# Decoder kernel of four layers: steps 20 to 37 of the closing chain one to four slots closer, last mixture opened at slot 90 instead of 94

## The reference, cut to what matters

```python
x = x + L2_xattn(layernorm(x), ctx, ctx)      # 16 heads, softmax, one output weight
x = x + L2_ffn(layernorm(x))                  # gated; fp4 quantised input, hidden and weights
x = x + L3_attn(layernorm(x))                 # linear: x @ q.T @ (x.T @ x)
x = x + L3_xattn(layernorm(x), ctx, ctx, ...) # no softmax, so keys x values is one 128x128; inner layernorm
x = x + L3_ffn(layernorm(x))                  # mixture: 8 experts 128 -> 512 -> 128, top 2 of 8, gelu
```

## Time and profile before

| what | us |
|---|---|
| median of three runs | 1243.61 (1237.75 to 1248.25) |
| the profiled execution | 1246.88 |
| its span in the trace | 1245.6 |
| outside the span | 1.3 |
| PE busy | 1028.6 (83%) |
| DVE busy | 800.2 (64%) |
| ACT busy | 612.5 (49%) |
| POOL busy | 252.0 (20%) |

### The profile page before, as it was taken

The page is one execution under the profiler, slowest core; times in us unless marked ns, Lnnn a source line. Parts: engine busy times, 40 slices in busy tenths (PEclk is TensorE's granted clock), DMA queues, the critical chain, the costliest instruction groups (busy, mean ns, idle before and its releaser), DMA issues.

```text
span 1245.6 us, 19903 instructions
## 1 busy us (share of the span) xinstructions
PE 1028.6 (83%) x7630; PEld 550.0 (44%) x7649; DVE 800.2 (64%) x2016; ACT 612.5 (49%) x1018; POOL 252.0 (20%) x309
## 2 busy tenths in 40 slices
PE   5777779999899974778867889999658868779999
PEld 4233313333667652345532333566412333437767
DVE  7786867751324467877777882677688887665412
ACT  2456436566433527678763777323115546433342
POOL 2833210000000225477551000001222001000000
PEclk9778869999999996566776997999858989879999
DMA  8323040000000210068013201700101200100000
GB/s 302 94 72 85 27 179 2 2 2 2 1 1 1 77 54 7 1 186 156 17 45 125 116 2 19 125 1 1 52 26 33 97 1 2 34 1 1 1 9 9
DMA packets 34785, 61.23 MB, mean 49 GB/s; under 512 B 4771, under 2 KB 25076, under 8 KB 33092
## 3 DMA queue, kind: packets, MB, share of 16 engines
q1 hardware_dynamic: 33828, 58.64, 16.7%
q10 hardware_dynamic: 864, 1.33, 0.3%
HBM read 42.91 MB, written 16.65 MB: 48 GB/s over the span
## 4 chain that ended last, share of the span: by engine, by line
PE 59%; DVE 27%; ACT 5%; issue 4%; POOL 3%; DMA 2%; SPq 1%; DVEq 0%; POOLq 0%; ACTq 0%
PE ps_s L879 10%; PE ps_e L869 9%; PE ps_v L672 6%; DVE mx L1864 6%; PE ps_e L608 5%; PE ps_s L629 3%; PE ps_e L606 3%; DVE ps_s L1860 2%; PE ps_e L973 2%; PE ps_s L960 2%; ACT work L1396 2%; DVE mx L1854 2%; DVE stats L1802 1%; DVE xn L1820 1%; PE ps_v L1144 1%
## 5 line engine op out<-in xcount | busy, mean ns | idle before, releaser
L1396 ACT ACTIVATE work<-ps_e 128x512 f32<-128x512 f32 x448 | 250.7, 598 | 148.1 <-PE ps_e L608 142.8
L2622 POOL TENSOR_TENSOR rstd<-rstd,halves 128x2 f32<-128x2 f32 x52 | 36.6, 704 | 699.0 <-DVE rstd L1807 698.8
L1864 DVE TENSOR_REDUCE mx<-ps_s 128x2 f32<-128x1024 f32 x128 | 154.1, 1222 | 27.8 <-PE ps_s L629 26.3
L629 PE MATMUL ps_s<-ctx_stack,q_stack 49*128 49x512 bf16 (+1 forms) x384 | 128.5, 453 | 47.1 <-DVE mx L1864 34.8
L608 PE MATMUL ps_e<-q_stack,ctx_stack 52*128 52x256 bf16 (+1 forms) x768 | 149.7, 297 | 16.8 <-issue 6.3
L1498 ACT ACTIVATE work<-ps_s,keep 128x512 f32<-128x512 f32 x136 | 93.1, 687 | 140.4 <-PE ps_s L879 137.5
L672 PE MATMUL ps_v<-work,vaug 128*32 128x256 f32 x1536 | 132.0, 420 | 4.8 <-ACT work L1384 4.8
L869 PEld LDWEIGHTS ps_e<-ffn_w,work 128*128 128x128 f32 x960 | 117.9, 196 | 21.0 <-issue 19.9
L879 PE MATMUL ps_s<-xnT,ffn_w 128*128 128x512 f32 x240 | 119.4, 623 | 3.6 <-ACT work L1498 3.6
L869 PE MATMUL ps_e<-ffn_w,work 128*128 128x128 f32 x960 | 119.7, 280 | 0.8 <-DVE x L2054 0.8
L2064 DVE SCALAR_TENSOR_TENSOR x<-ps_e,gates,x 128x128 f32<-128x128 f32 x128 | 38.9, 346 | 121.7 <-PE ps_e L869 118.7
(11 more groups left out here) (380 smaller groups left out, 1815.7 us busy)
## 6 DMA issues: line engine op xcount, KB each, us to landing
q_stack<-q_scr SPq DMA_DIRECT2D x32, 192.0 KB
ffn_w<-in_L0f_w SPq DMA_DIRECT2D x1, 4608.0 KB, 14.7
ffn_w<-in_L1f_w SPq DMA_DIRECT2D x1, 3456.0 KB, 13.1
q_scr<-parts SPq DMA_DIRECT2D x16, 192.0 KB, 2.1
c_scr<-ffn_w SPq DMA_DIRECT2D x12, 256.0 KB, 7.7
kx_scr<-ffn_w SPq DMA_DIRECT2D x12, 256.0 KB, 4.2
ctx_stack<-kx_scr SPq DMA_DIRECT2D x2, 1536.0 KB
ctx_stack<-c_scr SPq DMA_DIRECT2D x2, 1536.0 KB
```

Of the source, the lines that this page charges most:

```text
L629: return pe.matmul(ps_s[i][:, parity, :], q_stack[p0:p0 + n_rows, b, pair, part * P:(part + 1) * P], ctx_stack[p0:p0 + n_rows, pair, b * S ...
L1396: act.activation(pt[:, parity, :, :].rearrange("p k q -> p (k q)"), bank[f"e{parity}"], ACT.Exp).then_inc(exped, 1)
L1864: m = dve.tensor_reduce(mx[:, b, :, pair, part], ps_s[i][:], AX, ALU.max, negate=True)
```

## The change

A table STEP_AT gives each step its distance to the close slot. Steps up to 18 keep theirs; 20 to 37 come one to four slots sooner, 22 in the slot of 21. `chain_steps` goes by the table, and so do all counts. TAIL0 goes from 94 to 90, and every piece of the mixture comes four slots sooner. Since the cross attention still has steps in slots 90 to 92 (the close of batch 3), `l3_tail` now calls `cross_slot` too, behind the slot's pieces and ahead of its chain, with s1 alone.

```diff
+STEP_AT = {4: 4, 5: 5, 7: 7, 8: 8, 9: 9, 10: 10, 11: 11, 12: 12, 15: 15, 16: 16, 17: 17, 18: 18, 20: 19, 21: 20,
+           22: 20, 24: 21, 25: 22, 27: 23, 28: 24, 29: 25, 30: 26, 31: 27, 32: 28, 33: 29, 34: 30, 35: 31, 36: 32, 37: 33}
 CHAIN = [("L2f", 3), ("L3a", 17), ("L3x", 24), ("L3x-inner", 33), ("L3f", 34)]
-tail = sorted((close_slot(X2, b) + at, b, st) for st, at in CHAIN for b in range(B))
-tail = [(st, b) for _, b, st in tail]
+
+def chain_slot(b, at):
+    return close_slot(X2, b) + STEP_AT.get(at, at)
+
+tail = sorted((chain_slot(b, at), st != "L2f", b, at, st) for st, at in CHAIN for b in range(B))
+tail = [(st, b) for _, _, b, _, st in tail]
...
-LAST = {A0: 54, X0: 96, X1: 96, X2: 93, "chain": 125}
+LAST = {A0: 54, X0: 96, X1: 96, X2: 93, "chain": 121}
...
-TAIL0 = 94
+TAIL0 = 90
...
-PIECES_BEFORE = {95: 2, 96: 1, 97: 1, 98: 1, 99: 2, 101: 1, 102: 1, 103: 1, 104: 1, 105: 1, 106: 1, 107: 1, 108: 1, 109: 1,
...
+PIECES_BEFORE = {91: 2, 92: 1, 93: 1, 94: 1, 95: 2, 97: 1, 98: 1, 99: 1, 100: 1, 101: 1, 102: 1, 103: 1, 104: 1, 105: 1,
...
     def chain_steps(slot):
         for b in range(B):
-            yield b, slot - close_slot(X2, b)
+            for at in STEP_AT:
+                if chain_slot(b, at) == slot:
+                    yield b, at
...
                 n += PIECES_BEFORE.get(t, 0)
+                if t < LAST[X2]:
+                    cross_slot(X2, t, kp("L2x_T"), None, window_tile)
                 chain(t)
```

More of the change, by code:

```diff
@@ L140 @@
 TURNS = [("L2f", 7), ("L3a", 20), ("L3x", 27), ("L3f", 36)]
-turned_tail = sorted((close_slot(X2, b) + at, b, st) for st, at in TURNS for b in range(B))
-TURN_AT = order_of(front + [(st, b) for _, b, st in turned_tail])
+turned_tail = sorted((chain_slot(b, at), b, at, st) for st, at in TURNS for b in range(B))
+TURN_AT = order_of(front + [(st, b) for _, b, _, st in turned_tail])
 BEFORE = {"L2f": "L2x", "L3a": "L2f", "L3x": "L3a", "L3f": "L3x"}
@@ L150 @@
 CHAIN_PS = [17, 20, 22, 24, 33]
-PS_AT = order_of([(at, b) for _, b, at in sorted((close_slot(X2, b) + at, b, at) for at in CHAIN_PS for b in range(B))])
-LAST = {A0: 54, X0: 96, X1: 96, X2: 93, "chain": 125}
+PS_AT = order_of([(at, b) for _, b, at in sorted((chain_slot(b, at), b, at) for at in CHAIN_PS for b in range(B))])
+LAST = {A0: 54, X0: 96, X1: 96, X2: 93, "chain": 121}
 CFILL = {X0: 32, X1: 128, X2: 192}
@@ L231 @@
 ROUTE1 = len(PIECES) - 2
-PIECES_BEFORE = {95: 2, 96: 1, 97: 1, 98: 1, 99: 2, 101: 1, 102: 1, 103: 1, 104: 1, 105: 1, 106: 1, 107: 1, 108: 1, 109: 1,
-                 110: 1, 111: 1, 113: 1, 114: 2, 116: 1, 117: 1, 118: 1, 120: 1, 122: 2, 123: 2, 124: 1}
+PIECES_BEFORE = {91: 2, 92: 1, 93: 1, 94: 1, 95: 2, 97: 1, 98: 1, 99: 1, 100: 1, 101: 1, 102: 1, 103: 1, 104: 1, 105: 1,
+                 106: 1, 107: 1, 109: 1, 110: 2, 112: 1, 113: 1, 114: 1, 116: 1, 118: 2, 119: 2, 120: 1}
 L3F_OWN = 6
@@ L1538, in l3_tail @@
                 chain(t, False)
+                if t < LAST[X2]:
+                    cross_slot(X2, t, None)
                 chain(t, True)
@@ L2118, in l3_tail @@
                 n += PIECES_BEFORE.get(t, 0)
+                if t < LAST[X2]:
+                    cross_slot(X2, t, "L2f", window_tile)
                 chain(t)
```

## The result

The changed kernel takes 1253.32 us (median of 15 runs, 1249.97 to 1259.84), the kernel before beside it 1243.61 (15 runs, 1236.35 to 1254.59). The ratio is 1.0084, interval 1.0065 to 1.0104: slower by about 9.7 us. The forecast was 1242.9 with a range up to 1251, so both the value and the range were wrong, on the slow side. The profiled execution has a span of 1253.0 us, and PE's clock was granted at 0.864 on average.

A forecast was written before the change was run, and what follows sets the result against it. PE was taken as the bound from 1122.77 us on, with idle time and low clock to win between 1045 and 1123. Terms 0 + 1.0 - 3.2 + 1.5 = -0.7 us gave 1242.9 against the median 1243.61; range 1234 to 1251.

The forecast's parts named there:

- Slots 59 to 68: Batch 0 moved, DVE paced by the maxima, up to F': value 0, a wait of 0.8 us gone or come.
- F' to F: From batch 1's fp4 end (F') to batch 2's (F), slots 68 to 84: +1.0 us, from waits at steps 36 and 27.
- the 0.81 of the root is covered: Part of F' to F: with step 28 leaving DVE's fp4 block (0.60), it gives back 1.4 us.
- F to the first downs: From batch 2's fp4 end until twelve ups, gates and bias are done: F + 38.75 instead of F + 41.97, so -3.2 us.
- That clock held for 11.35 us of work; I take the same here: Step in F to the first downs: 11.35 us of work at the low clock, as before, 5.65 in full-speed units.
- From there to the end: Behind the first downs: waits of 2.3 us in slot 104 and 0.5 in slot 108, old waits gone; net +1.5 us.
- A third gap, and slower: Rival at L554 behind step 35 of batch 2, slot 104: clock falls there too, +7.4 us, 1251.0; chance 0.17.
- The clock stays up: Rival in slot 88: the wait is too short to drop the clock, -7.9 us, 1235.7; chance 0.17.
- The slots count: Rival in the tail: batch 3's chain, not PE's work, sets it; four slots fewer give -10.7 us, 1232.9; chance 0.06.
- signs of a wrong forecast: Clock under 1.00 behind the first downs, first up later than F + 15, or period between fp4 ends under 35 us.
- signs of being right: Step 36 waits 4 to 5 us in slots 72 and 88, DVE's holes gone, first up near F + 12, bias about 3.

The follow-up runs named there:

- Filled: Changed kernel with idle matmuls only ahead of the turns of step 27 (2 for batch 0, 4 for batch 1): 1247.14 us, ratio 1.0033.
- At one clock: Changed kernel with five waits filled by 29 idle matmuls (1240.99 us) beside the kernel before with its waits over 1 us behind slot 70 filled (1238.25 us).
- the filled kernel: Changed kernel, same order, with 29 idle matmuls in five waits (step 36 of batches 0, 1, 2; step 27 of batch 1; bias): 1240.99 us, ratio 0.9983.
- the experiment on before: Kernel before with idle matmuls at two waits only, 5 and 11 at the turns of step 36 of batches 0 and 1: 1243.89 us, ratio 1.0009.
- three other runs: Changed kernel with steps 27 to 37 one slot later (1240.22 us), with only step 27 filled (1247.14 us), with only step 36 filled (1247.71 us).

## Why the prediction was wrong, point by point

- *What bounds the kernel.* Right in the place: the difference arose almost wholly where PE has slack and a clock below 1.00. Its clock was named there, but I had read it from long stretches and so missed two of its four falls. The mechanism, waits that move and a clock that falls at them, was the right one; their sizes and number were not.
- *Slots 59 to 68: value 0, bounds ±0.8.* The stretch up to F' grew by 2.0 us. What failed is "PE wants the normalised tile of step 25 one slot after DVE makes it instead of two", priced as a wait of at most 0.8 with nothing for the clock. It came as 1.00 + 0.47, inside a fall that had begun at the maxima and that lasted 10.3 us instead of 3.6. Filled, the stretch is +0.2 (46.31 against 46.13).
- *F' to F: +1.0, bounds -1.4 and +3.4.* This is the term that failed most: +6.45. At one clock the order costs +2.8, inside the bounds, so taking the middle was 1.8 too low. Two of its parts were wrong. Step 36's wait was forecast at 4.1 and was 2.68, near the old 2.49: the turn came 6.70 us behind F', as counted (6.55), but PE was occupied for 4.0 us of it and not 2.5, as the sum had left out its wait of 1.02 for ACT's lift. And "the 0.81 of the root is covered", a gain, came as two more uncovered roots, 1.6 us of DVE's waits. Step 27's wait, up to 1.8, was 2.07. The other 3.6 us are the clock, which I had priced at nothing: the second wait of the period, in slot 79, lets it fall once more.
- *F to the first downs: -3.2, bounds -8.9 and +1.5.* It came as -0.5. The first up was forecast near F + 12 and stands at F + 11.74, the bias wait was forecast at 3.2 and is 3.41. The step "That clock held for 11.35 us of work; I take the same here" failed in form: the first fall held for 7.5 us of work, and a second one, behind the bias wait (1114.4 to 1121.2), for 6.2 more. In its sum it was nearly right: the clock's price was put at 5.65 us, and filling the waits gives 5.06 back. What was mis-sized by more is the rest. At full clock the forecast would have been 38.75 - 5.65 = 33.1 us, and the filled kernel takes 36.38. Its waits behind the turn are some 8.9 us where I had 6.1: 1.32 at the third up instead of 0.7, 0.83 at step 7 instead of 0.5, 3.5 of filled wait at the bias, and two I had not seen, 1.14 at the closing out-projection (L603, behind ACT, whose gelus are queued ahead of its part of the close) and 0.37 at the gram.
- *From there to the end: +1.5.* It came as +2.2; the wait in slot 104 was forecast at 2.3 and is 2.63. At one clock the order costs only +0.6 here; the other 1.6 is the clock behind that wait (0.64 over the slice from 1144), in a stretch that ran at 1.00.
- *The rivals.* "A third gap, and slower" (1251.0, chance 0.17) is what happened, in kind: the place was L564 behind step 35 of batch 2, and the clock fell there. But this was the shortest of the falls in the changed kernel; most of the added time at the low clock comes from slots 63 and 79. The argument against it, that "waits of 1.9 and 1.7 us before 1122.7 left the clock alone", was the weak point. Those two rows were one execution; in the experiment on before, a wait of the same 1.91 us was followed by 0.59 over 7.7 us. Its argument for it, that a standing of 2.49 us sufficed, was no safer: 2.20, 2.63 and 2.65 left the clock at 1.00 in three other runs. The Trainium skill, "TensorE: Matmul & The Clock Gate", section "HAM oscillation — how this bites in real kernels", says that the price is paid again at each gap. I had cited it and then applied it to one more gap only; the changed kernel agrees with it at all five waits of over 2 us, the three runs just named don't at theirs. "The clock stays up" and "The slots count" did not occur: opening four slots sooner changed the time by no more than the noise (1257.07 against 1253.32).
- *What would show it.* One of the three signs of a wrong forecast came, a clock under 1.00 behind the first downs (0.64). The period between fp4 ends went to 42.6 us, but my sign was one shorter than 35; I had set no sign for a longer one. Of the signs of being right, the first up near F + 12 and the bias wait near 3 us came all the same; the turns of step 36 waited 2.68 and 3.85 us instead of 4 to 5.

In one sentence: the change's order costs at one clock 2.1 us from F' on where the sum said -0.7, and the clock, priced as two falls whose cost stays the same, fell six times instead of four and cost 6.0 us more there and most of the 2.0 in front of it.

## What to carry to other kernels

Where PE runs in order through a stretch in which another engine is the bound, take each wait above some 1 us as standing plus a possible spell at half clock (one fall here followed waits of 0.47 and 0.75 us only), count such waits before and after a move, and widen the range by what the falls may cost; whether a given wait brings one changed from run to run here. The other engine's busy sum tells nothing of it (DVE: 23.83 and 23.88 us). Before judging a reordering by its time, fill the waits of both orders with idle matmuls: at one clock the comparison shows the order's own worth (+2.1 us from F' on, for a change that measured +9.7 in all). Filling the waits of a whole stretch is itself a gain (7.5 us in the kernel before), filling some of them need not be.

## What the runs showed of the hardware

- Which wait is followed by a fall is not decided by its length alone. The wait of 1.91 us at the bias left the clock at 1.00 in the kernel before and was followed by 0.59 over 7.7 us in one that differs only in idle matmuls elsewhere. The wait in slot 104, 2.63 to 2.65 us, was followed by a fall in the changed kernel (0.64) and left the clock at 1.00 in two that differ from it only in idle matmuls elsewhere. A wait of 2.20 us (1048.72, steps 27 to 37 one slot later) left it at 1.00 too. Whether the work around the waits or the moment decides isn't separated by these runs.
- A later wait can prolong a fall that has begun: behind the wait of 1.5 us for the maxima the fall lasted 10.3 us with waits of 1.00 and 0.47 inside it, and 3.6 and 3.4 us in the two kernels without the wait of 1.00.
- A semaphore wait of PE costs more than its length when it ends in the low clock: with 29 idle matmuls (0.45 us each in a run of eight) in five waits the same order took 12.3 us less.
- Idle matmuls in front of a wait need not delay it: behind sixteen records that took 3.62 us the turn in slot 88 still waited 0.32 us for DVE.
